# A graph attention layer and a mixture of experts on one core: another order of one step's work in the attention stage

## The chip, the cores and the metric

The kernel runs as one program on one core of a Trainium2 chip. The core has TensorE (PE: matmuls, with a separate path for loading weights, PEld), VectorE (DVE), ScalarE (ACT), GpSimd (POOL) and SyncE (SP, which here issues all the DMAs). Each engine works through its own queue in the order in which it was written, and semaphores tie the queues together. The metric is the device time of one execution in microseconds.

## The reference, cut to what matters

The input is 128 graphs of 128 nodes with 256 features each, and a weighted adjacency matrix for each graph. All is float32.

```
x = x + gnn(layernorm(x), adj, W, a)
x = x + ffn(layernorm(x), ...)

gnn: Wh = h @ W;  s1 = Wh @ a1;  s2 = Wh @ a2
     e = leaky_relu(s1[i] + s2[j], 0.2) + log(adj + 1e-6)
     h' = softmax(e) @ Wh

ffn: w = softmax(mean over graphs(h) @ Wr + br)          # 8 experts
     for each expert: relu(bn(h @ W1 + b1)), relu(bn(. @ W2 + b2)), . @ Wo + bo
     y = sum of the experts' results, weighted by w
```

## The kernel before, in words

The program has two stages. The first, the attention stage, goes through 32 groups of four graphs and leaves x + h' of each group in a buffer in device memory. The second goes through the same groups as tiles of 512 rows and computes the eight experts. The change touches the first stage alone.

In the attention stage each engine runs the function `step(g, layer)` for g from -1 to 33 in a software pipeline. In step g the engines work on several groups: `nxt` is group g+1, g itself, `a` is group g-1, `b` is g-2, `t` is g-3 and `h` is g-4. The journey of one group is this:

- `nxt`: TensorE transposes its rows (L774, into `ps_th`), ScalarE copies them (`xnT`, L530). VectorE takes the mean and variance of each row (`stats_1`, L559, aggregated at L573), and GpSimd makes the reciprocal deviation (L399, L403).
- g: TensorE projects (`project`, L726, into `ps_wide`), ScalarE copies with the deviation as scale (`wh`, L512). TensorE spreads the score of each node over the partitions (L765, into `ps_s`), ScalarE adds the other score (`s_sb`, L520).
- `a`: VectorE makes the leaky ReLU (`l_sb`, L617) and the negated row maximum (L627), ScalarE the exponential (`e_sb`, L504), VectorE the product with the adjacency matrix (`p_sb`, L661) and its row sums (L674).
- `b`: TensorE transposes p_sb (L737, into `ps_pT`), ScalarE copies it (`pT`, L497), TensorE multiplies it with wh (the attention product, L755, into `ps_th`), and VectorE divides by the row sums and adds the rows of x (`x1`, L647). It then takes the statistics of the new rows (L567).
- `t` and `h`: the statistics are aggregated (L578), GpSimd makes the deviation (L433, L436), and the normalised rows are summed over the groups in `acc`, which is `resb`: two of the four graphs on VectorE (`add_part`, L604), two on GpSimd (`x1s_high` L442, and the addition L446).

The rows of x, transposed, and the attention product use the same PSUM tensor (`ps_th`), and the two copies of wh alternate between groups, so that the copy of wh of group g overwrites the wh that the attention product of group g-2 reads.

The order of the work is written out by hand in `step` of each engine. Three ranges of steps differ in what they do on the side. Steps -1 to 5 and 30 to 33 are unrolled and do nothing else. Steps 6 to 21 (`layer == 1`, a loop of pairs) prepare the first weights of one expert in each pair: in the even step SyncE loads W1 into `w_stage` and GpSimd makes four sums of blocks of it (L455 to L462); in the odd step ScalarE copies them to a rounded form (`wq_hi`, L541) and GpSimd takes the rest (`wq_lo`, L467). Steps 22 to 29 (`layer == 2`) prepare the second weights, one expert in each step: SyncE loads W2 (L366) into one half of `w_stage`, ScalarE copies it (`w_hi`, L545), GpSimd takes the rest (`w_lo`, L472).

SyncE issues in step g: the rows of x of group g+2 (L326, which wait for the transposes and the row statistics of group g), the store of group g-3 (L347), the rows of x of group g-1 once more, for the sum (L352), the adjacency matrices of group g (L355), and the weights if there are any.

Of the kernel before, what the change touches and what calls it, by code (L numbers as in the profile page):

```python
# [24 lines left out]
P = 128  # L25
# [13 lines left out]
def adj_ffn(nc, x, adj, gnn_w, gnn_a, wr, br, w1, b1, g1, be1, m1, v1, w2, b2, g2, be2, m2, v2, wo, bo, out):  # L39
# [17 lines left out]
    with ExitStack() as ctx:  # L57
# [127 lines left out]
        with ExitStack() as sa:  # L185
# [296 lines left out]
            def _(act):  # L482
# [8 lines left out]
                def step(g, layer):  # L491
                    p = g[1]
                    b = ago(g, 2)
                    if exists(b):
                        act.wait_ge(pT_ready, num(b) + 1)
                        wait(act, h_ready, num(b))
                        nc.scalar.activation(pT[:, :, :], ps_pT[:, :, :], ACT.Copy).then_inc(pT_copied, 1)  # L497
                    a = ago(g, 1)
                    if exists(a):
                        act.wait_ge(neg_m_done, num(a) + 1)  # L500
                        wait(act, p_done, num(a))

                        for b4 in range(GB):
                            last = nc.scalar.activation(e_sb[:, b4, :], l_sb[:, b4, :], ACT.Exp,  # L504
                                                        bias=neg_m[:, b4:b4 + 1])
                        last.then_inc(e_done, 1)
                    if exists(g):
                        act.wait_ge(wh_ready, num(g) + 1)
                        act.wait_ge(rstd1_done, num(g) + 1)
                        wait(act, h_ready, num(g) - 1)  # L510
                        for b4 in range(GB):
                            last = nc.scalar.activation(wh[p][:, b4, :], ps_wide[:, b4, 0:D + 2], ACT.Copy,  # L512
                                                        scale=rstd1[p][:, b4:b4 + 1])
                        last.then_inc(wh_copied, 1)
                    nxt = ago(g, -1)
                    if exists(g):
                        act.wait_ge(s2b_ready, num(g) + 1)
                        wait(act, l_done, num(g))
                        for b4 in range(GB):
                            last = nc.scalar.activation(s_sb[:, b4, :], ps_s[:, b4, :], ACT.Identity,  # L520
                                                        bias=wh[p][:, b4, D:D + 1])
                        last.then_inc(s_done, 1)
                    if is_step(g, BN_STEP - 1):
                        act.wait_ge(bn_T, 1)
                        nc.scalar.activation(bn_in[:, :, :, :].rearrange("p l i k -> p (l i) k"), ps_bn,
                                             ACT.Copy).then_inc(bn_copied, 1)
                    if exists(nxt):
                        act.wait_ge(xnT_ready, num(nxt) + 1)
                        wait(act, wh_ready, num(nxt))
                        nc.scalar.activation(xnT[:, :, :], ps_xT, ACT.Copy).then_inc(xnT_copied, 1)  # L530
                    t = ago(g, 3)
                    if exists(t) and not is_step(t, G - 1):
                        act.wait_ge(stats2_done, num(t) + 1)
                        nc.scalar.activation(mean_all[:, num(t), :], mv2[t[1]][:, :, 0],
                                             ACT.Copy).then_inc(mean2_done, 1)
                    if is_step(g, G):
                        tile_copy(act, 0, ps_x0)
# [4 lines left out]
                    if layer == 2:  # L542
# [3 lines left out]
                                             w_half[p], ACT.Copy).then_inc(w_hi_done, 1)  # L546

# [5 lines left out]
            def _(dve):  # L553
# [31 lines left out]
                def step(g, layer):  # L585
# [23 lines left out]

                    if exists(b):  # L610
                        dve.wait_ge(rowsum_done, num(b) + 1)
# [12 lines left out]
                    add_part(0)  # L624
# [4 lines left out]
                    add_part(1)  # L629
# [23 lines left out]
                    if exists(nxt):  # L653
                        wait(dve, rstd1_done, num(nxt) - 1)
                        stats_1(nxt, 0)
                        stats_1(nxt, 1)
# [7 lines left out]
                    if exists(nxt):  # L664
                        stats_1(nxt, 2)
                        stats_1(nxt, 3)
# [32 lines left out]
            def _(pe):  # L699
# [30 lines left out]
                def step(g, layer):  # L730
                    b = ago(g, 2)
                    nxt = ago(g, -1)
                    if exists(b):
                        pe.wait_ge(p_done, num(b) + 1)
                        wait(pe, pT_copied, num(b))
                        for b4 in range(GB):
                            last = nc.tensor.transpose(ps_pT[:, b4, :], p_sb[:, b4, :], ident[:, :])  # L737
                        last.then_inc(pT_ready, 1)
                    if is_step(g, G):
                        pe.wait_ge(wh_copied, G)  # L740
                        tile_transpose(pe, 0, ps_x0)
                    if is_step(g, 0):
                        pe.wait_ge(va_copied, 1)
                    if exists(g):
                        pe.wait_ge(xnT_copied, num(g) + 1)
                        wait(pe, wh_copied, num(g))
                        project(g, range(GB)).then_inc(wh_ready, 1)
# [530 lines left out]
```

## Time and profile before

| what | value |
|---|---|
| median of three runs | 2516.02 us (2515.35 to 2516.1) |
| the profiled execution's own time | 2515.62 us |
| its span | 2513.8 us |
| PE busy | 2397.0 us (95%) |
| DVE busy | 1729.6 us (69%) |
| ACT busy | 1596.0 us (63%) |
| POOL busy | 453.7 us (18%) |
| attention stage | from the start to about 370 us |

The busy times are sums over the whole span, of which the attention stage is about a seventh, so they say little about it; its own steps have to be read from the timeline. In the rows of the timeline a line gives the start, the duration, the engine, the line of the kernel, the instruction, what it writes and reads, and how many instructions in succession were merged into the row. A bracket at the end gives the time that the engine sat idle before the row, and what ended it. A row of windows gives the stretch, its length, the busy time and instructions of PE, PEld, DVE, ACT and POOL, and then TensorE's granted clock, the DMA engines' busy share and GB/s.

### The profile page before, as it was taken

What the parts mean: (1) busy time and instruction counts of PE and PEld (TensorE: products, weight loads), DVE (VectorE), ACT (ScalarE), POOL (GpSimd) and SP (SyncE); (2) the same over time, 40 slices, a digit from 0 to 9 for tenths busy, and PEclk for the clock granted to TensorE, in tenths of its full rate; (3) what the DMA queues carried; (4) which work ended last, traced back from release to release, by engine and by line L of the source; (5) the groups of instructions that cost most, each with busy time, mean ns of one, the idle gap of its engine ahead of it and who ended that gap; (6) DMA issues with size and microseconds to landing.
All of it is one profiled execution on the core that took longest, in us unless ns stands there. A gap on an engine that the chain in (4) does not pass through costs nothing.

```text
span 2513.8 us, 45142 instructions
## 1 busy us (share of the span) xinstructions
PE 2397.0 (95%) x16308; PEld 2209.6 (88%) x16308; DVE 1729.6 (69%) x2445; ACT 1596.0 (63%) x2465; POOL 453.7 (18%) x423
## 2 busy tenths in 40 slices
PE   6777769999999999999999999999999999999999
PEld 5666648999999999999999999999999999999998
DVE  4888875666666666666666666666666666666665
ACT  3555545666666666666666666666666666666665
POOL 3566642111101110111111111111111001101110
PEclk9999988999999999999999999999999999999999
DMA  4555641000000000000000000000000000000000
GB/s 136 192 187 187 199 133 43 26 26 25 25 25 25 23 19 23 18 18 25 25 25 25 25 25 25 25 25 25 25 25 25 25 25 25 17 25 17 17 18 26
DMA packets 91179, 116.16 MB, mean 46 GB/s; under 512 B 4701, under 2 KB 78857, under 8 KB 91145
## 3 DMA queue, kind: packets, MB, share of 16 engines
q1 hardware_dynamic: 91144, 115.73, 14.0%
q8 instruction: 19, 0.31, 0.1%
q14 instruction: 16, 0.12, 0.0%
HBM read 82.16 MB, written 33.55 MB: 46 GB/s over the span
## 4 chain that ended last, share of the span: by engine, by line
PE 84%; DVE 1%; ACT 0%; issue 0%; ACTq 0%
PE ps_y L1178 29%; PE ps_wide L171 29%; PE ps_wide L1160 26%; PE ps_t L132 1%; DVE h_lo L1065 0%; DVE h L1072 0%; PE ps_y L1226 0%; DVE z L1058 0%; ACT v L972 0%; DVE h_lo L1080 0%; ACT h_hi L986 0%; ACT h_hi L967 0%; ACT w_bc L1014 0%; ACT h L980 0%; DVE z L1048 0%
## 5 line engine op out<-in xcount | busy, mean ns | idle before, releaser
L972 ACT ACTIVATE v<-ps_wide,bn_cols 128x256 f32<-128x256 f32 x768 | 434.6, 566 | 399.1 <-PE ps_wide L1160 272.1
L980 ACT ACTIVATE h<-ps_wide,bn_cols 128x512 f32<-128x512 f32 x512 | 399.3, 780 | 328.4 <-PE ps_wide L171 328.4
L1178 PE MATMUL ps_y<-wo_lo,h_hi 128*128 128x256 f32 x2048 | 578.8, 283 | 0.0
L1178 PE MATMUL ps_y<-wo_hi,h_hi 128*128 128x256 f32 x2048 | 577.1, 282 | 1.6 <-DVE h_lo L1080 1.6
L1178 PE MATMUL ps_y<-wo_hi,h_lo 128*128 128x256 f32 x2048 | 578.3, 282 | 0.0
L1160 PE MATMUL ps_wide<-xq_hi,wq_hi 128*128 128x256 f32 x1792 | 505.9, 282 | 11.9 <-PEq L185 8.4
L1160 PE MATMUL ps_wide<-xq_lo,wq_hi 128*128 128x256 f32 x1792 | 509.5, 284 | 0.0
L1160 PE MATMUL ps_wide<-xq_hi,wq_lo 128*128 128x256 f32 x1792 | 506.8, 283 | 0.0
L1080 DVE TENSOR_TENSOR h_lo<-h,h_hi 128x1024 fp32r<-128x1024 f32 x256 | 318.1, 1243 | 241.6 <-ACT h_hi L986 241.6
L1058 DVE SCALAR_TENSOR_TENSOR z<-ps_wide,bn_cols,v 128x512 f32<-128x512 f32 x256 | 192.0, 750 | 319.3 <-PE ps_wide L1160 319.3
L171 PE MATMUL ps_wide<-h_hi,w_hi 128*128 128x512 f32 x1024 | 404.8, 395 | 2.1 <-DVE h_lo L1065 2.1
L171 PE MATMUL ps_wide<-h_lo,w_hi 128*128 128x512 f32 x1024 | 405.9, 396 | 0.0
L171 PE MATMUL ps_wide<-h_hi,w_lo 128*128 128x512 f32 x1024 | 405.9, 396 | 0.0
L1065 DVE SCALAR_TENSOR_TENSOR h_lo<-z,h_hi 128x1024 fp32r<-128x1024 f32 x256 | 316.3, 1235 | 117.9 <-ACT h_hi L967 117.9
L1178 PEld LDWEIGHTS ps_y<-wo_hi,h_hi 128*128 128x128 f32 x2048 | 386.5, 189 | 1.9 <-DVE h_lo L1080 1.8
L1178 PEld LDWEIGHTS ps_y<-wo_hi,h_lo 128*128 128x128 f32 x2048 | 387.4, 189 | 0.0
L1178 PEld LDWEIGHTS ps_y<-wo_lo,h_hi 128*128 128x128 f32 x2048 | 386.4, 189 | 0.1
L950 POOL TENSOR_TENSOR resb<-resb,bias_out 128x1024 f32<-128x1024 f32 x32 | 85.6, 2674 | 1535.2 <-DMA resb<-x_scratch 1535.2
L1160 PEld LDWEIGHTS ps_wide<-xq_hi,wq_hi 128*128 128x128 f32 x1792 | 340.9, 190 | 24.6 <-issue 9.4
L1160 PEld LDWEIGHTS ps_wide<-xq_hi,wq_lo 128*128 128x128 f32 x1792 | 338.2, 189 | 10.0
L1160 PEld LDWEIGHTS ps_wide<-xq_lo,wq_hi 128*128 128x128 f32 x1792 | 339.8, 190 | 0.0
L1072 DVE TENSOR_TENSOR h<-h,w_bc 128x1024 f32<-128x1024 f32 x256 | 313.1, 1223 | 7.5 <-ACT w_bc L1014 4.7
(131 smaller groups left out, 3059.4 us busy)
## 6 DMA issues: line engine op xcount, KB each, us to landing
x_sb<-in_x SPq DMA_DIRECT2D x32, 512.0 KB, 3.9
res<-in_x SPq DMA_DIRECT2D x32, 512.0 KB, 5.8
x1t<-x_scratch SPq DMA_DIRECT2D x32, 512.0 KB, 3.3
resb<-x_scratch SPq DMA_DIRECT2D x32, 512.0 KB, 3.3
out<-resb SPq DMA_DIRECT2D x32, 512.0 KB, 3.0
adj_sb<-in_adj SPq DMA_DIRECT2D x32, 256.0 KB, 6.0
x_scratch<-h SPq DMA_DIRECT2D x16, 512.0 KB, 4.7
x_scratch<-w_bc SPq DMA_DIRECT2D x16, 512.0 KB, 4.5
```

What stands on the lines that cost most here:

```text
L132: last = nc.tensor.transpose(ps_x[:, c, b4 * N:(b4 + 1) * N], x1t[:, b4, c * P:(c + 1) * P], ident[:, :])
L171: mm = nc.tensor.matmul(acc_ps, w[:, i, c, cols], s[:, c, :], start=start and n == 0, stop=stop and n == len(terms) - 1)
L950: nc.gpsimd.tensor_tensor(resb[:, :, :], resb[:, :, :], bias_out[:, None, :].to_broadcast([P, GB, D]), ALU.add).then_inc(resb_done, 1)
L972: nc.scalar.activation(v[:, slot, :], ps_l1[:, 0, 0:H], ACT.Identity, bias=bn_cols[:, 1, cols], scale=bn_cols[:, 0, cols]).then_inc(done, 1)
L980: nc.scalar.activation(h2[:, m, :], ps_l2[:, m, :], ACT.Relu, bias=bn_cols[:, 3, cols], scale=bn_cols[:, 2, cols]).then_inc(r2_done, 1)
L1058: nc.vector.scalar_tensor_tensor(out=z[:, 0, :], in0=ps_l1[:, 1, :], scalar=bn_cols[:, 0, C * e:C * e + 1], in1=v[:, 0:2, :].rearrange("p ...
L1065: nc.vector.scalar_tensor_tensor(out=h1_lo[:, :, :], in0=z[:, :, :], scalar=0.0, in1=h1_hi[:, :, :].bitcast(F32), op0=ALU.max, op1=ALU.sub ...
L1072: nc.vector.tensor_tensor(h2w[:, :, :].rearrange("p c (b n) -> p (c b) n", n=N), h2[:, :, :].rearrange("p c (b n) -> p (c b) n", n=N), w_b ...
L1080: nc.vector.tensor_tensor(h2_lo[p][:, :, :], h2w[:, :, :], h2_hi[p][:, :, :].bitcast(F32), ALU.subtract).then_inc(lo2_done, 1)
L1160: mm = nc.tensor.matmul(out_ps, w[:, e, q, :], x[:, q, :], start=start and n == 0, stop=stop and n == len(terms) - 1, skip_group_check=True)
L1178: mm = nc.tensor.matmul(ps_y[:, b4, :], h[:, c, cols], w[:, e, c, :], start=(e == 0 and k == 0 and b4 % per_bank == 0), stop=(e == E - 1 a ...
```

## The change

In the attention stage the queues of TensorE, ScalarE and VectorE get another order in `step`. No instruction is added or taken away, and the other queues stay as they are.

- TensorE had: transposes of p_sb (of group g-2), projection, attention product, spread scores, transposes of the next rows. It now has: attention product (g-2), projection (g), transposes of the next rows (g+1), spread scores (g), and last the transposes of p_sb, now of group g-1.
- ScalarE had: pT (g-2), exp (g-1), wh (g), s (g), xnT (g+1), the means, weights. It now has: s (now of group g-1), the weights, exp (g-1), the means, wh (g), xnT (g+1), and last pT (now of group g-1).
- VectorE has both additions to `acc` at the head of the step, ahead of the leaky ReLU, and all four row statistics of the next group behind p_sb.

```
# TensorE, step
-                    if exists(b):
-                        pe.wait_ge(p_done, num(b) + 1)
-                        wait(pe, pT_copied, num(b))
-                        ... transposes of p_sb into ps_pT ...
                     if exists(b):
                         pe.wait_ge(pT_copied, num(b) + 1)
-                        pe.wait_ge(wh_copied, num(b) + 1)
                         wait(pe, x1_done, num(b))
                         ... attention product ...
+                    if exists(g):
+                        ... project(g) ...
+                    if exists(nxt):
+                        pe.wait_ge(x_loaded[nxt[1]], 16 * (nxt[0] + 1))
+                        for c in range(C):
+                            wait(pe, (x1_low_done, x1_done)[c], num(b) + 1)
+                            ... transposes of the next rows ...
                     if exists(g):
                         ... spread scores ...
-                    if exists(nxt):
-                        ... transposes of the next rows ...
+                    if exists(a):
+                        pe.wait_ge(p_done, num(a) + 1)
+                        wait(pe, pT_copied, num(a))
+                        ... transposes of p_sb into ps_pT ...
# ScalarE, step
-                    if exists(b):
-                        ... pT ...
                     a = ago(g, 1)
+                    if exists(a):
+                        act.wait_ge(s2b_ready, num(a) + 1)
+                        wait(act, l_done, num(a))
+                        ... s_sb, with wh of a ...
+                    if layer == 1 and p == 1:
+                        ... wq_hi, behind wq_sum ...
+                    if layer == 2:
+                        act.wait_ge(w2_loaded[p], 16 * (g[0] - K1 + 1))
+                        ... w_hi ...
                     if exists(a):
                         ... e_sb ...
+                    ... mean_all ...
                     if exists(g):
                         ... wh ...
-                    if exists(g):
-                        ... s_sb, with wh of g ...
                     if exists(nxt):
                         ... xnT ...
-                    ... mean_all, wq_hi, w_hi ...
+                    if exists(a):
+                        act.wait_ge(pT_ready, num(a) + 1)
+                        wait(act, h_ready, num(a))
+                        ... pT ...
# VectorE, step
+                    add_part(0)
+                    add_part(1)
                     ... l_sb, rinv, aggregate_2 ...
-                    add_part(0)
                     ... neg_m ...
-                    add_part(1)
                     ... x1 ...
-                    stats_1(nxt, 0), stats_1(nxt, 1)
                     ... p_sb ...
-                    stats_1(nxt, 2), stats_1(nxt, 3)
+                    stats_1(nxt, 0) to stats_1(nxt, 3)
                     ... stats_2, rowsum, aggregate_1 ...
```

## Rows read from the trace of the kernel before

**Rows 1.** Timeline of VectorE: p_sb in steps 1, 6, 29 and 32.
```profile
29.17 0.69 DVE L661 SCALAR_TENSOR_TENSOR p_sb<-adj_sb,e_sb 128x512 f32<-128x512 f32 x1 [0.69 <-ACT e_sb L504]
...
85.50 0.67 DVE L661 SCALAR_TENSOR_TENSOR p_sb<-adj_sb,e_sb 128x512 f32<-128x512 f32 x1
...
326.69 0.68 DVE L661 SCALAR_TENSOR_TENSOR p_sb<-adj_sb,e_sb 128x512 f32<-128x512 f32 x1
...
354.66 1.47 DVE L661 SCALAR_TENSOR_TENSOR p_sb<-adj_sb,e_sb 128x512 f32<-128x512 f32 x1
```
**Rows 2.** Timeline of TensorE, steps 16 and 17.
```profile
190.39 1.16 PE L765 MATMUL ps_s<-ident,wh 128*128 128x128 f32 x8 [1.67 <-ACT wh L512]
...
191.38 1.04 PE L774 MATMUL ps_th<-ident,x_sb 128*128 128x128 f32 x8
...
192.25 0.60 PE L737 MATMUL ps_pT<-ident,p_sb 128*128 128x128 f32 x4
...
193.69 3.76 PE L726 MATMUL ps_wide<-gw,xnT 128*128 128x258 f32 x16 [0.84 <-ACT xnT L530]
...
197.29 1.89 PE L755 MATMUL ps_th<-wh,pT 128*128 128x256 f32 x8
```
**Rows 3.** Timeline of ScalarE in the same stretch.
```profile
191.58 1.15 ACT L520 ACTIVATE s_sb<-ps_s,wh 128x128 f32<-128x128 f32 x4 [1.25 <-PE ps_s L765]
...
193.60 0.62 ACT L497 ACTIVATE pT<-ps_pT 128x512 f32<-128x512 f32 x1
...
196.12 1.28 ACT L504 ACTIVATE e_sb<-l_sb,neg_m 128x128 f32<-128x128 f32 x4 [1.89 <-DVE neg_m L627]
...
199.30 1.58 ACT L512 ACTIVATE wh<-ps_wide,rstd 128x258 f32<-128x258 f32 x4 [1.91 <-PE ps_th L755]
```
**Rows 4.** Timeline of VectorE from p_sb of step 16 to that of step 17.
```profile
190.48 0.67 DVE L661 SCALAR_TENSOR_TENSOR p_sb<-adj_sb,e_sb 128x512 f32<-128x512 f32 x1
...
194.07 0.69 DVE L617 SCALAR_TENSOR_TENSOR l_sb<-s_sb 128x512 f32<-128x512 f32 x1
...
195.03 0.45 DVE L604 SCALAR_TENSOR_TENSOR resb<-w_bc,rstd_all,resb 128x256 f32<-128x256 f32 x1
...
196.00 0.61 DVE L604 SCALAR_TENSOR_TENSOR resb<-w_bc,rstd_all,resb 128x256 f32<-128x256 f32 x1
...
198.45 1.66 DVE L647 SCALAR_TENSOR_TENSOR w_bc<-ps_th,rinv,res 128x256 f32<-128x256 f32 x4 [1.84 <-PE ps_th L755]
...
200.69 0.72 DVE L661 SCALAR_TENSOR_TENSOR p_sb<-adj_sb,e_sb 128x512 f32<-128x512 f32 x1
```
**Rows 5.** Timeline of GpSimd, and one addition of VectorE, in steps 16 to 18.
```profile
194.45 0.63 POOL L455 TENSOR_TENSOR w_stage<-w_stage 128x128 f32<-128x128 f32 x1
...
196.41 0.52 POOL L462 TENSOR_TENSOR w_stage<-w_stage 128x128 f32<-128x128 f32 x1
...
198.47 1.04 POOL L442 TENSOR_TENSOR x1s_high<-h,rstd_all 128x512 f32<-128x512 f32 x1 [0.18 <-POOL rstd_all L436]
...
205.31 2.08 POOL L467 TENSOR_TENSOR wq_lo<-w_stage,wq_hi 128x896 f32 x1 [0.59 <-ACT wq_hi L541]
...
205.39 2.29 DVE L604 SCALAR_TENSOR_TENSOR resb<-h,rstd_all,resb 128x256 f32<-128x256 f32 x1
```
**Rows 6.** SyncE's first and last issue in step 25, w_stage's landings, w_hi.
```profile
276.60 0.37 SPq L326 DMA_DIRECT2D x_sb<-in_x  x1
...
279.84 0.42 SPq L366 DMA_DIRECT2D w_stage<-in_L_ffn_W  x1
...
DMA to landing us min/median/max: 3.7/5.3/5.8
...
288.14 0.65 ACT L545 ACTIVATE w_hi<-w_stage 128x512 f32 x1
```
**Rows 7.** TensorE's transposes of p_sb in step 33, and that stretch by windows.
```profile
356.19 1.11 PE L737 MATMUL ps_pT<-ident,p_sb 128*128 128x128 f32 x4 [3.21 <-DVE p_sb L661]
...
356.00:362.00 6.00, 4.89 (x12) 3.24 (x12) 4.32 (x16) 0.80 (x2) 3.10 (x5) 0.50 0.16 65
```

More of the change, by code:

```diff
@@ L507, in step @@
-                    if exists(g):
[L508 to L514, printed above, removed]
@@ L531, in step @@
[L531 to L537, printed above, removed]
                     if layer == 1 and p == 1:
@@ L664, in step @@
                     if exists(nxt):
-                        stats_1(nxt, 2)
-                        stats_1(nxt, 3)
+                        wait(dve, rstd1_done, num(nxt) - 1)
+                        for b4 in range(GB):
+                            stats_1(nxt, b4)
                     if with_stats:
@@ L759, in step @@
                         last.then_inc(h_ready, 1)
+                    if is_step(g, 0):
+                        pe.wait_ge(va_copied, 1)
+                    if exists(g):
+                        pe.wait_ge(xnT_copied, num(g) + 1)
+                        wait(pe, wh_copied, num(g))
+                        project(g, range(GB)).then_inc(wh_ready, 1)
+                    if is_step(g, G):
+                        pe.wait_ge(wh_copied, G)
+                        tile_transpose(pe, 0, ps_x0)
+                    if exists(nxt):
+                        pe.wait_ge(x_loaded[nxt[1]], 16 * (nxt[0] + 1))
+                        for c in range(C):
+                            wait(pe, (x1_low_done, x1_done)[c], num(b) + 1)
+                            for b4 in range(GB):
+                                last = nc.tensor.transpose(ps_xT[:, c, b4 * N:(b4 + 1) * N],
+                                                           x_sb[nxt[1]][:, b4, c * P:(c + 1) * P], ident[:, :])
+                        last.then_inc(xnT_ready, 1)
                     if exists(g):
@@ L767, in step @@
                         last.then_inc(s2b_ready, 1)
-                    if exists(nxt):
-                        pe.wait_ge(x_loaded[nxt[1]], 16 * (nxt[0] + 1))
-                        wait(pe, xnT_copied, num(nxt))
-                        for c in range(C):
-                            wait(pe, (x1_low_done, x1_done)[c], num(b) + 1)
-                            for b4 in range(GB):
-                                last = nc.tensor.transpose(ps_xT[:, c, b4 * N:(b4 + 1) * N],
-                                                           x_sb[nxt[1]][:, b4, c * P:(c + 1) * P], ident[:, :])
-                        last.then_inc(xnT_ready, 1)
+                    if exists(a):
+                        pe.wait_ge(p_done, num(a) + 1)
+                        wait(pe, pT_copied, num(a))
+                        for b4 in range(GB):
+                            last = nc.tensor.transpose(ps_pT[:, b4, :], p_sb[:, b4, :], ident[:, :])
+                        last.then_inc(pT_ready, 1)
                     if is_step(g, BN_STEP - 1):
```

69 lines of the change are left out of this document (31 added, 38 removed).

## The prediction

> **What bounds the kernel now.** I read the page first: the slices show the attention stage in the first seventh of the span (the change touches nothing else), and the chain of waits lies almost wholly in the stage behind it, so it doesn't price this change. I then read the timeline of two neighbouring steps in the middle of the stage, engine by engine, and last what the DMA queue and GpSimd do in the steps that also load weights. I mark a step by the start of its product p_sb (L661): 85.50 us in step 6, 326.69 in step 29, so 23 steps took 241.2 us, 10.49 each [rows 1].
>
> One step closes a loop through TensorE and ScalarE [rows 2, 3]: projection to the start of the attention product 3.60 us (193.69 to 197.29), product 1.89, then the copies of wh 1.58, which wait for that product (its wait is printed on the row), the broadcast 1.16, and the copies of s and xnT 2.11 (191.58 to 193.69, where the projection starts, its wait for xnT printed on the row); with 0.2 of hand-overs 10.54. VectorE is a near second: from p_sb at 190.48 to the next at 200.69 it waited only 1.84, for the product [rows 4]. So 8.2 us of its own work stand in a lap (3.59 to l_sb, then 6.62 less 1.84 and less 0.16 that one addition lost).
>
> **The change, part by part.** Times below are counted from T, the start of a step's attention product.
>
> TensorE's order. Nothing is added. The product goes first and its pT was copied in the step before, so wh no longer waits for a product behind the projection. Lap: product 1.73 of its 1.89 (the next instruction starts before the last one ends, as the 0.99 from 190.39 to 191.38 of 1.16 show), projection 3.76, wh copies 1.58 (the transposes of the next rows, 0.87, lie beside them), broadcast 0.99 to the first transpose of the product, transposes 0.60, copy of pT 0.62 [rows 2, 3], four hand-overs 0.18: 9.46. The copies of s now run at the head of the next step beside the product, xnT's copy beside the broadcast, and neither is waited for. That is 1.08 less than 10.54. What is late next is VectorE: its transposes need p_sb at T+8.15.
>
> VectorE's order. The two additions (0.45 each, 0.4 apart) now stand ahead of l_sb, the four row statistics behind p_sb. The moves cost no instruction. l_sb starts at T+1.1 (s ready), the maximum and x1 follow (1.93 to the second addition, less the first, 0.4; then 1.6), so p_sb is reached 3.1 after l_sb, T+4.2; exp, 1.28 after the maximum, is hidden by x1 [rows 3, 4]. x1 is done at T+4.2, before the row transposes want it (T+5.3). The reserve toward T+8.15 is 3 us, and toward the wh copies behind exp on ScalarE 1.3.
>
> The port that VectorE and GpSimd share. An addition of 0.45 took 2.29 beside GpSimd's wq_lo (2.08), and ended 0.29 after it [rows 4, 5]: of two instructions one waits for the other's end. In the new order p_sb meets GpSimd's x1s_high (1.04), which starts 1.5 after GpSimd turns to the aggregated variance (196.93 to 198.47), l_sb+2.6 to +3.65. So p_sb loses between 0 and 1.04; I take 0.35, nearest to these starts. VectorE's lap is then 8.55, below 9.46: plain steps run at 9.46. From p(0) at 29.2 (unchanged, [rows 1]): wh 1.6, broadcast 1.0, transposes 0.6, copy 0.7, so T of step 2 is 33.15; four laps of 9.46 later step 6 has T 71.0 and p_sb at 75.4, 10.1 earlier than now.
>
> Steps 6 to 21 (one W1 expert per pair). GpSimd reaches its weight work 3.97 after p_sb (190.48 to 194.45); with two statistics (0.65, 2.24 less x1's 1.6) now behind p_sb, 4.62 [rows 4, 5]. VectorE's second addition starts at p_sb+4.65 and l_sb wants to at 5.05. In the odd step that weight work is wq_lo, 2.08: the addition or l_sb waits it out, so l_sb starts at p_sb+6.85. In the even step it is the first of four sums, about 0.3: l_sb at p_sb+5.25. Their end, 2.1 after l_sb's start (196.93 less 194.07 is 2.9 today, with both additions between), releases wq_hi (0.97, estimated from w_hi's 0.65 for 512 columns against 896), which now stands ahead of exp: exp ends 4.4 after l_sb and p_sb starts at 4.5. GpSimd, freed by the same sum, is then just ending x1s_high. A pair is odd 4.5+6.85, even 3.45+5.25, together 20.05 against 20.97 now; VectorE is the bound, TensorE's 18.92 is hidden. Both ends: 18.92 (all hidden) and 22.4 (GpSimd's addition behind x1s_high, 1.2 by an estimate from the 1.04 of that one, also goes ahead of p_sb, once in each step). 15 steps at 10.0: p_sb of step 21 at 225.4 against 242.8.
>
> Steps 22 to 29 (one W2 expert each): here the change loses. ScalarE's w_hi stood at the end of its step (288.14), on weights whose load was issued at 279.84; its median landing is 5.3, so it had 3.0 of cover [rows 6]. It now stands behind s, at T+1.1, ahead of exp, wh, xnT and pT. SyncE issues that load last of five in its step, 3.24 behind the load of x_sb (276.60), and x_sb's load waits for the row statistics, now behind p_sb. So a loop closes: p_sb 0.67, four statistics 1.35, hand-over to SyncE 0.2 (an estimate), four issues 3.24, landing 5.3, w_hi 0.65, exp 1.28, hand-overs 0.14: 12.8 us, against 10.49. That the engines idle in it changes nothing. Its ends: landing 3.7 (the one issued apart from the others) gives 11.2, landing 5.8 gives 13.3. I take 5.3, since the four transfers ahead on the same queue are unchanged. The first of the eight is issued behind wq_lo instead (p_sb+7.3) and lands in 3.7: 13.0 with w_hi and exp. p_sb of step 29: 225.4+13.0+7*12.8=328.0 against 326.7.
>
> TensorE's clock in these steps. Now its longest wait in a step is 1.67 [rows 2]. In the new loop the row transposes end at T+6.3 and the broadcast starts after exp and wh, T+10.5: 4.2 us idle in 12.8. After 3.21 us of idleness four transposes took 1.11 instead of 0.60 and the granted clock was 0.50, the 1.2 GHz level [rows 7]. One step at that level costs the others nothing, since p_sb hangs on the load with 4 us in reserve; only the broadcast and transposes of step 29 (1.6 at full clock, 0.85 of that more) would pass on: 0 to 1.4, and I take 1.4. The Trainium skill (TensorE: Matmul & The Clock Gate, section "Why this matters for your kernels") says that idle gaps between bursts of matmuls bring back the half clock, which speaks against this change: by it the drop is certain, and the steps behind would start slow too (about what the second rival gives). The trace agrees in kind [rows 7].
>
> The end. Behind step 29: 3.9 to T of step 30, two laps of 9.46, and 4.4 to p_sb of step 32: 27.2, against 28.8 now (354.66 plus 0.80 by which its 1.47 exceed 0.67, less 326.69). Two additions (0.8) come ahead of the aggregation from which the stage's end hangs. So 328.0+27.2+0.8-355.5=0.5, and the clock's 1.4: +1.9 us.
>
> The profiled execution took 2515.62 (span 2513.8), 0.4 below the median 2516.02. 2515.6+1.9+0.4=2518.
>
> **The rivals.**
> 1. The W2 load is less in the way: the loop of steps 22 to 29 takes 11.2 with the 3.7 landing. For it: the queue has longer pauses between bursts. Against: the burst in front of the load is the same four transfers. 8*1.6=12.8 less: 2505, faster.
> 2. TensorE falls to the half clock in steps 22 to 29 and stays there for several. For it: 4.2 us of idleness against the 3.21 of [rows 7]. Against: at half clock TensorE would be busy nearly throughout, which should bring the clock back. Its lap would be (1.73+3.76+0.99+0.60)*1.85+2.4=15.5, 2.7 over the loop; in five of eight steps 13: 2531, slower. It decides from the point where the late TensorE exceeds p_sb's reserve, after two such steps.
> 3. GpSimd wins the port in each step, its addition as well as x1s_high running ahead of p_sb: VectorE's lap is 9.75 in plain steps (1 in all), and 1.2 more in each of 15: 2537, slower. Against it: at wq_lo's end (207.39) the waiting VectorE instruction went ahead and ended at 207.68 [rows 5].
> 4. The change doesn't shorten the plain laps (s at the head of ScalarE's step runs into something unseen): 10 lost, 2528. Little speaks for it.
>
> **How the numbers follow.** Forecast 0.52, own range 2511 to 2525; rivals 0.24, 0.15, 0.06, 0.03. Two gains of about 10 and 7 us are set against a loss of 19, so the sign is open; 0.2% (5 us) is about what this kernel's measurement tells from no change. The forecast gives 0.08 faster, 0.28 same, 0.16 slower; rival 1 gives 0.22 faster and 0.02 same, the others slower but 0.01. So faster 0.30, same 0.31, slower 0.39. The range is 2503 to 2534: below by rival 1 with a little more from the port, above by rival 2.
>
> **What would show it.** p_sb 9.4 to 9.5 apart in steps 3 to 6; about 20 us per pair in steps 6 to 21, with l_sb (or an addition) of 2 us and more beside wq_lo; 12.8 apart in steps 22 to 29, with w_hi and exp waiting for the DMA of w_stage; x_sb's issues right behind the statistics. Wrong if w_hi doesn't wait, if TensorE's clock is 0.50 through those steps, or if p_sb takes over 1.5 us in most steps.

## The result, and the profile after

The kernel after took 2512.56 us (median of 20 runs, 2510.76 to 2516.51), the kernel before beside it 2516.59 (20 runs, 2515.29 to 2518.15): ratio 0.9985 with a 95% interval of 0.9979 to 0.9992. It is faster by 4 us, where 1.9 slower was forecast. The profiled execution of after took 2514.45 (span 2512.7), 1.2 less than that of before. The rest of the 4 us is scatter of single executions, which is wider than before (5.8 us from lowest to highest, against 2.9): the profiled execution of after lies 1.9 above its median, that of before 1.0 below. The profiled executions of stats_ahead, stats_ahead_warm and adds_back, further down, lie 4.4 below, 4.8 above and 2.5 above their medians, so a difference of a few us between two rows of the table can be scatter.

The small sum hides two large terms. I take them from the starts of p_sb (now L656), which is the mark the prediction uses. In the timeline of VectorE, steps 21, 22, 29 and 30 of after (start us, duration, engine, line, operation, and in brackets the idle time before it and what ended it):

```profile
219.01 0.83 DVE L656 SCALAR_TENSOR_TENSOR p_sb<-adj_sb,e_sb 128x512 f32<-128x512 f32 x1 [1.19 <-ACT e_sb L515]
...
231.54 0.69 DVE L656 SCALAR_TENSOR_TENSOR p_sb<-adj_sb,e_sb 128x512 f32<-128x512 f32 x1 [4.35 <-ACT e_sb L515]
...
325.17 0.69 DVE L656 SCALAR_TENSOR_TENSOR p_sb<-adj_sb,e_sb 128x512 f32<-128x512 f32 x1 [3.92 <-ACT e_sb L515]
...
334.56 0.98 DVE L656 SCALAR_TENSOR_TENSOR p_sb<-adj_sb,e_sb 128x512 f32<-128x512 f32 x1
```

With the same marks of every kernel run for this study (us of its profiled execution, all starts of p_sb, read from timelines; step 29 and 32 of before are [rows 1]):

```
                  step 21    21 to 29 (a lap)   29 to 32   step 32
before             242.69     84.00 (10.50)      27.97     354.66
forecast           225.4     102.6  (12.8)       27.2+1.4  356.6
after              219.01    106.16 (13.27)      28.25     353.42
w_hi_last          219.25     75.73  (9.47)      27.60     322.58
stats_ahead        221.70     89.65 (11.21)      29.07     340.42
load_first         219.48     82.03 (10.25)      28.24     329.75
adds_back          236.68    102.50 (12.81)      32.93     372.11
warm               218.81    104.16 (13.02)      28.17     351.14
stats_ahead_warm   221.96    100.05 (12.51)      27.00     349.01
dve_only           242.79     83.99 (10.50)      28.45     355.23
wq_early           217.85     76.88  (9.61)      27.61     322.34
pe_act_only        226.50     97.13 (12.14)      31.70     355.33
adds_back_wq       221.88    102.82 (12.85)      31.71     356.41
load_fourth        219.78     99.09 (12.39)      29.94     348.81
```

After has gained 23.7 us by step 21, and has lost 22.2 of it again by step 29.

**Plain steps.** TensorE and the two copies that end its waits, step 3 to 4 of after:

```profile
41.76 1.99 PE L736 MATMUL ps_th<-wh,pT 128*128 128x256 f32 x8 [0.69 <-ACT pT L543]
...
43.60 3.65 PE L722 MATMUL ps_wide<-gw,xnT 128*128 128x258 f32 x16
...
47.29 1.58 ACT L528 ACTIVATE wh<-ps_wide,rstd 128x258 f32<-128x258 f32 x4 [0.90 <-PE ps_wide L722]
...
48.91 1.16 PE L763 MATMUL ps_s<-ident,wh 128*128 128x128 f32 x8 [0.79 <-ACT wh L528]
...
49.91 0.60 PE L770 MATMUL ps_pT<-ident,p_sb 128*128 128x128 f32 x4
...
50.55 0.60 ACT L543 ACTIVATE pT<-ps_pT 128x512 f32<-128x512 f32 x1 [0.77 <-PE ps_pT L770]
...
51.20 0.48 PE L736 MATMUL ps_th<-wh,pT 128*128 128x256 f32 x1 [0.69 <-ACT pT L543]
```

Each row starts within 0.2 us of where the one above ends, product to product 9.44 (51.20 less 41.76). This is the lap that the prediction added up from the rows of before. The starts of p_sb are 9.0 to 9.4 apart in laps 4 to 6, since VectorE has reserve and its own mark moves inside TensorE's lap.

**Steps 6 to 21.** From step 9 on the starts of p_sb repeat every four laps (8.11, 9.69, 10.35, 10.07, in all 38.22, 9.56 each); over all fifteen laps they are 9.66 apart, while TensorE's products are 9.55 apart (70.14 in step 6, 213.38 in step 21), so that p_sb slides 1.6 us back inside TensorE's lap. Two neighbouring odd steps differ. GpSimd, VectorE and TensorE, steps 14 to 16:

```profile
165.51 2.26 POOL L467 TENSOR_TENSOR wq_lo<-w_stage,wq_hi 128x896 f32 x1
...
165.59 1.99 PE L736 MATMUL ps_th<-wh,pT 128*128 128x256 f32 x8 [0.76 <-ACT pT L543]
166.52 1.79 DVE L618 SCALAR_TENSOR_TENSOR l_sb<-s_sb 128x512 f32<-128x512 f32 x1 [0.70 <-ACT s_sb L498]
...
175.17 1.99 PE L736 MATMUL ps_th<-wh,pT 128*128 128x256 f32 x8 [0.76 <-ACT pT L543]
...
184.72 1.99 PE L736 MATMUL ps_th<-wh,pT 128*128 128x256 f32 x8 [0.77 <-ACT pT L543]
185.03 0.86 DVE L603 SCALAR_TENSOR_TENSOR resb<-h,rstd_all,resb 128x256 f32<-128x256 f32 x2
185.58 2.86 POOL L467 TENSOR_TENSOR wq_lo<-w_stage,wq_hi 128x896 f32 x1
185.81 0.68 DVE L618 SCALAR_TENSOR_TENSOR l_sb<-s_sb 128x512 f32<-128x512 f32 x1
```

In one, l_sb stands beside wq_lo and takes 1.79 instead of 0.68. In the other l_sb takes 0.68 and it is wq_lo that takes longer, 2.86. TensorE's products are 9.58 and 9.55 apart in spite of both, each waiting only for pT: VectorE's delays don't reach them. The 0.1 over the plain lap lies in the hand-overs (0.76 before the product instead of 0.69).

**Steps 22 to 29.** What was waited for on each engine, 220 to 330 us (us in total, times, longest):

```profile
ACT w_hi L508 <- DMA w_stage<-in_L_ffn_W: 48.1, 8, 7.1
...
DVE p_sb L656 <- ACT e_sb L515: 32.0, 8, 4.7
PEld ps_s L763 <- ACT wh L528: 26.1, 9, 5.3
```

The chain from one p_sb to the next, timeline of step 22 to 23 (SPq are SyncE's issues):

```profile
232.15 1.40 DVE L558 BATCH_NORM_STATS2 st<-x_sb 128x6 f32<-128x256 f32 x4
...
233.78 0.37 SPq L326 DMA_DIRECT2D x_sb<-in_x  x1
...
237.00 0.47 SPq L366 DMA_DIRECT2D w_stage<-in_L_ffn_W  x1
...
243.49 0.63 ACT L508 ACTIVATE w_hi<-w_stage 128x512 f32 x1 [7.11 <-DMA w_stage<-in_L_ffn_W]
244.02 1.26 ACT L515 ACTIVATE e_sb<-l_sb,neg_m 128x128 f32<-128x128 f32 x4
245.31 0.69 DVE L656 SCALAR_TENSOR_TENSOR p_sb<-adj_sb,e_sb 128x512 f32<-128x512 f32 x1 [4.66 <-ACT e_sb L515]
246.88 2.08 PE L763 MATMUL ps_s<-ident,wh 128*128 128x128 f32 x8 [5.07 <-ACT wh L528]
```

That is the loop of the prediction, here 13.77 long: the row statistics release x_sb's load, SyncE issues the W2 load 3.2 later, and this landed 6.4 after its issue, not 5.3. In the seven full laps (22 to 29) every other part is fixed within 0.4 us: 2.2 from p_sb to x_sb's issue, 3.2 to 3.6 to the W2 load's issue, 1.83 from w_hi to the next p_sb. Only the time from that issue to w_hi moves, 5.3 to 7.0, 6.0 on average. The last row also shows TensorE at its lower level of 1.2 GHz, 2.08 for what takes 1.16, behind 5.07 of idleness. By windows (start:end, length, busy time of TensorE, its weight loads, VectorE, ScalarE and GpSimd, granted clock, DMA share, GB/s):

```profile
80.00:225.00 145.00, 121.00 (x670) 102.93 (x670) 131.46 (x412) 89.66 (x236) 110.09 (x130) 1.00 0.64 205
238.00:330.00 92.00, 67.74 (x298) 56.34 (x296) 58.33 (x189) 40.13 (x108) 41.82 (x49) 0.80 0.51 164
```

No engine is near full in the second window, and neither are the DMA engines over a whole lap (0.51): a chain of waits sets the time there. One link of it, the landing, is the length of a burst, in which the DMA engines are busy (last section).

### The profile page after: what moved, and what is told of

Its sections match the earlier page's. It is cut to its first block, busy times and chain, and to the rows that moved or that the text cites. A ratio compares the mean times of both kernels' runs of the same rounds, so it can differ in the third digit from the quotient of the medians.

```text
span 2512.7 us, 45085 instructions
## 1 busy us (share of the span) xinstructions
PE 2410.9 (96%) x16308; PEld 2222.2 (88%) x16308; DVE 1717.6 (68%) x2445; ACT 1594.9 (63%) x2465; POOL 459.1 (18%) x423
## 4 chain that ended last, share of the span: by engine, by line
PE 84%; DVE 1%; ACT 0%; issue 0%; ACTq 0%
PE ps_y L1173 29%; PE ps_wide L171 29%; PE ps_wide L1155 26%; PE ps_t L132 1%; DVE h_lo L1060 0%; DVE h L1067 0%; PE ps_y L1221 0%; DVE z L1053 0%; ACT v L967 0%; DVE h_lo L1075 0%; ACT h_hi L981 0%; ACT h_hi L962 0%; ACT w_bc L1009 0%; ACT h L975 0%; DVE z L1043 0%
```

## Experiments

I had two questions. Is the loss in steps 22 to 29 the place of w_hi, or TensorE's clock? And what sets the laps up to step 21: VectorE with the port (my theory), or TensorE's loop? Ratios are to the kernel before on the same chip, with 95% intervals. All kernels compute the whole reference.

**w_hi_last**: after, with w_hi back at the end of ScalarE's step.

```
# ScalarE, step
-   ... w_hi, behind s_sb ...
    ... e_sb, mean_all, wh, xnT, pT ...
+   ... w_hi ...
```

> The changed kernel with the copy w_hi (W2 steps, 22 to 29) back at the end of ScalarE's step; all else as changed. Theory (load loop: the load of w_stage, w_hi, exp, p_sb, row statistics, the issue of x_sb's load, three more issues, the load): the wait of w_hi for the DMA goes from 48 us in eight steps to about 0, the p_sb of steps 22 to 29 come 9.4 to 9.7 apart instead of 13.3, TensorE's granted clock is 1.00 there, and the kernel takes 8*3.7=29 us less than the changed one: about 2484. Rival (the loss in these steps comes from VectorE and GpSimd meeting at the port, w_lo beside l_sb): w_lo is still there, laps stay above 12, about 2510.

Measured: 2485.10 (2483.32 to 2486.34, 4 runs), ratio 0.9877 [0.986, 0.9893]. Laps of 9.47 in steps 22 to 29, a granted clock of 1.00 (228 to 304 us), and no wait for the DMA of w_stage is left. The timeline of step 25 to 26:

```profile
262.78 0.47 SPq L366 DMA_DIRECT2D w_stage<-in_L_ffn_W  x1
...
270.69 0.62 ACT L542 ACTIVATE w_hi<-w_stage 128x512 f32 x1
```

The load has 7.9 us before it is wanted, more than the 5.4 median (6.0 at most) that it takes. So the place of this one copy costs 27 us of the change, and everything else in it is a gain of 31. This is the fastest order found, with wq_early within the scatter of it.

**stats_ahead**: after, with the four row statistics ahead of p_sb, so that x_sb's load is released earlier.

```
# VectorE, step
    ... x1 ...
+   stats_1(nxt, 0) to stats_1(nxt, 3)
    ... p_sb ...
-   stats_1(nxt, 0) to stats_1(nxt, 3)
```

> The changed kernel with the four row statistics ahead of p_sb; w_hi stays ahead of exp. Load-loop theory: the issue of x_sb's load no longer hangs on p_sb but on TensorE's row transposes, so the loop runs over two steps: exp's end to the next T 3.9, to the transposes' end 6.3, issue 0.2, three more issues 3.24, landing 5.5, w_hi 0.65, exp 1.28: 21.1 in two steps, 10.5 per lap in steps 22 to 29 instead of 13.3; w_hi still waits for the DMA. 22 us less than the changed kernel, about 2491. Rival (the half clock of TensorE makes these laps long): the clock would have to stay low, laps 12 and more, above 2505.

Measured: 2505.71 (2501.33 to 2506.85, 5 runs), 0.9957 [0.9943, 0.9971]. The sign was right and the size wrong: laps from 9.86 to 13.26, mean 11.21. Two of the eight were long (13.16 and 13.26), and in the lap ahead of each TensorE's product took 3.78 instead of 1.99 (236.21 and 260.24). Row transposes and x_sb's issue came late behind it, 2.6 and 3.1 after p_sb, where in the other full laps the issue lay between 1.1 ahead of p_sb and 0.6 behind it. The second of the two, by the timeline of step 24 to 25:

```profile
256.21 0.69 DVE L660 SCALAR_TENSOR_TENSOR p_sb<-adj_sb,e_sb 128x512 f32<-128x512 f32 x1 [2.16 <-ACT e_sb L515]
258.43 0.46 SPq L366 DMA_DIRECT2D w_stage<-in_L_ffn_W  x1
260.24 3.78 PE L736 MATMUL ps_th<-wh,pT 128*128 128x256 f32 x8 [0.76 <-ACT pT L543]
...
264.66 0.63 ACT L508 ACTIVATE w_hi<-w_stage 128x512 f32 x1 [3.51 <-DMA w_stage<-in_L_ffn_W]
```

The half clock is thus a second suspect for the long laps; warm and stats_ahead_warm take that up.

**load_first**: after, with SyncE issuing the W2 load first in its step, not last.

```
# SyncE, step
+   ... W2 load into w_half[p], with its two waits ...
    ... x_sb, x_scratch, res, adj_sb ...
-   ... W2 load ...
```

> The changed kernel, but SyncE issues the load of W2 first in its step instead of last; w_hi stays ahead of exp. Load-loop theory: the load no longer waits for the row statistics nor stands behind four other transfers, so it has landed before w_hi wants it: laps of 9.4 to 9.7 in steps 22 to 29, about 2484, as with w_hi at the end. Rival (w_hi's place on ScalarE ahead of exp is what costs, load or no load): laps stay above 12, about 2510.

Measured: 2490.79 (2489.27 to 2492.11, 4 runs), 0.9898 [0.9882, 0.9915]. Behind the first three laps (12.65, 9.87, 11.51) the laps are 9.5 to 9.7, and w_hi waited once, 6.0 us, where it waited 8 times for 48.1. With the load early, w_hi may stay where the change put it. The 7 us over my 2484 are those first laps. The first load can only be issued once wq_lo has freed w_stage (227.40), so w_hi waited 6.0 for it. TensorE, idle for 3.94 meanwhile, then ran at its lower level (the broadcast 2.08 at 233.69, the projection 4.46 at 240.96, granted clock 0.76 and 0.81 in 226 to 238 and 238 to 250 us), and the copy of wh waited 3.93 for that projection: here slow matmuls do stand in the way, for some 1.6 us (laps 9.87 and 11.51 against 10.22 and 9.52 in w_hi_last).

**adds_back**: after, with the two additions in their old places, behind aggregate_2 and behind neg_m.

```
# VectorE, step
-   add_part(0)
-   add_part(1)
    ... l_sb, rinv, aggregate_2 ...
+   add_part(0)
    ... neg_m ...
+   add_part(1)
    ... x1 ...
```

> The changed kernel with the two additions to acc in their old places, behind the aggregation and behind the maximum. Theory (in steps 3 to 21 TensorE's own loop of 9.44 us sets the lap and VectorE has about 1 us of reserve in each): the additions now stand between l_sb and p_sb, p_sb moves 0.8 later in its step and still comes before its transposes; laps in steps 6 to 21 stay within 9.5 to 9.7, steps 22 to 29 stay at 13.3; within 3 us of the changed kernel, 2510 to 2516. Rival (VectorE and the port set the lap in steps 6 to 21): wq_lo then meets two additions ahead of the maximum instead of one instruction, laps grow by 0.4 or more on average, 2519 and more.

Measured: 2531.12 (2528.44 to 2533.66, 4 runs), 1.0055 [1.0039, 1.0072], slower than both kernels and outside what my theory gave; the rival that priced the additions' place higher held. The laps of steps 6 to 21 are 10.68 long. Timeline of adds_back:

```profile
177.30 2.08 POOL L467 TENSOR_TENSOR wq_lo<-w_stage,wq_hi 128x896 f32 x1
177.38 2.54 DVE L616 SCALAR_TENSOR_TENSOR l_sb<-s_sb 128x512 f32<-128x512 f32 x1 [0.54 <-ACT s_sb L498]
...
182.77 1.35 PE L755 MATMUL ps_th<-ident,x_sb 128*128 128x128 f32 x8 [0.85 <-DVE h L646]
```

In every pair wq_lo starts ahead of l_sb, which loses 0.8 to 1.9 (here 1.85). With an addition on each side of neg_m, x1 then comes so late that TensorE's row transposes wait for it: here VectorE does set TensorE's pace. At the head of the step the additions run while VectorE would wait for s, and l_sb comes off wq_lo in every second pair.

**dve_only**: before, with VectorE's new queue alone.

```
# VectorE, step: additions to the head, all four statistics behind p_sb, as in after
# TensorE and ScalarE: as in before
```

> The kernel before, with only VectorE's new order (both additions at the head of the step, the four row statistics behind p_sb); TensorE and ScalarE as before. Theory (before, TensorE and ScalarE's loop of 10.54 sets the lap and VectorE waits in it for the product): laps stay 10.4 to 10.6, w_hi doesn't wait for the load; 2514 to 2519. Rival (the gain in steps 6 to 21 comes from VectorE's order by itself): laps of 10.1 or less there, 2510 or less.

Measured: 2515.83 (10 runs), 0.9997 [0.9987, 1.0006], laps of 10.49 and 10.50. Alone it does nothing, since the old loop through TensorE and ScalarE (10.54 by [rows 2, 3]) stays.

**pe_act_only**: the counterpart, TensorE's and ScalarE's new orders with VectorE's old queue.

```
# VectorE, step: additions at their old places, two statistics ahead of p_sb, two behind, as in before
# TensorE and ScalarE: as in after
```

> The new order on TensorE and ScalarE alone; VectorE's queue as in the kernel before (additions behind the aggregation and behind the maximum, two of the row statistics ahead of p_sb). Theory (the shorter loop of TensorE pays in steps 6 to 21 only with the additions at the head of VectorE's step, as the kernel with the additions back showed): laps there 10.4 to 10.8, in steps 22 to 29 11.5 to 13 with w_hi waiting for the load; 2520 to 2532, slower than before. Rival (the additions' place matters only together with the statistics behind p_sb): laps of 9.8 or less in steps 6 to 21, 2512 or less.

Measured: 2516.25 (10 runs), 1.0000 [0.999, 1.0009]. Of my numbers only the laps of steps 22 to 29 (12.14) held: 2520 to 2532 was too slow, and so were laps of 10.4 to 10.8, where 9.95 were measured. The rival's 9.8 and 2512 were not reached either. By the marks it gained 16.2 by step 21 (laps of 9.10 and 10.80), lost 13.1 in steps 22 to 29 and 3.7 behind them, +0.7 in all. Its loss in the load loop is smaller than that of after (97.13 against 106.16), as two statistics ahead of p_sb release x_sb's load earlier. Timeline:

```profile
170.91 2.08 POOL L467 TENSOR_TENSOR wq_lo<-w_stage,wq_hi 128x896 f32 x1
171.65 1.89 DVE L616 SCALAR_TENSOR_TENSOR l_sb<-s_sb 128x512 f32<-128x512 f32 x1 [1.20 <-ACT s_sb L498]
```

Behind step 29 a term shows that the prediction doesn't have. With the additions on both sides of neg_m the four normalisations of x1t (L124), which follow in step 31, take 3.1 us (before, pe_act_only, adds_back and adds_back_wq), with the additions at the head 1.4 (after). Why isn't shown.

pe_act_only and adds_back differ only in two row statistics, ahead of p_sb or behind it, and are 15 us apart (2516.25 and 2531.12); l_sb loses 1.2 beside wq_lo in the one and 1.9 in the other, but I didn't follow the rest.

So the whole change's 4 us are not the sum of its parts (0 and 0): VectorE's new queue is worth 0 on the old loop and 4 on the new one (7.5 by step 21).

**adds_back_wq**: adds_back, with wq_lo moved on GpSimd from behind the four sums to ahead of rstd_1, where VectorE has no l_sb.

```
# GpSimd, step (beside the edit of adds_back)
    ... x1s_high, addition ...
+   ... wq_lo ...
    ... rstd_1, transform of the weights ...
-   ... wq_lo ...
```

> The kernel with the additions back (2531.1, laps of 10.68 in steps 6 to 21, l_sb 2.5 us beside wq_lo in every pair), with GpSimd's wq_lo ahead of the deviation of the next rows, where VectorE runs the row statistics. Theory (the port makes the difference: additions between l_sb and x1 leave l_sb to meet wq_lo): no l_sb over 1 us, laps of 9.9 or less in steps 6 to 21, 2519 or less. Rival (x1 comes 0.8 later because of the additions themselves, and the row transposes and wh wait for it): laps stay at 10.3 or more, 2525 or more.

Measured: 2517.88 (10 runs), 1.0006 [0.9997, 1.0016], laps of 9.77 in steps 6 to 21, step 21 at 221.88 instead of adds_back's 236.68. Of these 14.8 us 1.3 were there at step 6, ahead of any wq_lo, so taking the meeting of l_sb and wq_lo away is worth 13.5 us in fifteen laps. l_sb took 1.00 at most, and theory and number held: where VectorE is late, the meeting counts.

**wq_early**: w_hi_last, with the same move of wq_lo.

```
# GpSimd, step (beside the edit of w_hi_last): wq_lo ahead of rstd_1
```

> The kernel with w_hi at the end of ScalarE's step (2485.1), and with GpSimd's wq_lo ahead of the deviation of the next rows instead of behind it, so that it runs beside the row statistics and not beside l_sb. Theory (in steps 6 to 21 TensorE's loop of 9.44 is the bound, and the port costs 0.2 per lap through l_sb's 1.8 us in every fourth step): no l_sb of over 1 us, laps 9.44 to 9.5 on average, 3 us less: 2482. Rival (VectorE's own work, not the port, holds the laps at 9.66): laps unchanged, 2485.

Measured: three runs of 2483.6 to 2488.1 (a fourth took 4776 and isn't counted), 0.9885 [0.9865, 0.9904], no better than w_hi_last. l_sb never took over 0.70:

```profile
165.71 1.99 PE L736 MATMUL ps_th<-wh,pT 128*128 128x256 f32 x8 [0.77 <-ACT pT L538]
166.64 0.69 DVE L618 SCALAR_TENSOR_TENSOR l_sb<-s_sb 128x512 f32<-128x512 f32 x1 [0.78 <-ACT s_sb L498]
...
175.29 1.99 PE L736 MATMUL ps_th<-wh,pT 128*128 128x256 f32 x8 [0.76 <-ACT pT L538]
176.40 0.69 DVE L618 SCALAR_TENSOR_TENSOR l_sb<-s_sb 128x512 f32<-128x512 f32 x1 [1.13 <-ACT s_sb L498]
...
184.79 1.99 PE L736 MATMUL ps_th<-wh,pT 128*128 128x256 f32 x8 [0.76 <-ACT pT L538]
```

Its laps are 9.95 and 9.13, 9.54 each, against 9.56 with the meetings; the products stand 9.58 and 9.50 apart. Taking the suspected bound away moved the settled lap by 0.02 us, and TensorE's products by 0.01 (9.54 apart from step 6 to 21, against 9.55 in after and w_hi_last). p_sb of step 21 does come 1.4 us earlier than in w_hi_last, as it no longer slides back inside TensorE's lap, but that is reserve and not time. My 2482 and the rival's 2485 are too close for three runs to tell apart. This is the run that fells "VectorE is the bound": TensorE's loop is.

**warm**: after, with TensorE repeating the transposes of the next rows four times in steps 22 to 29. The repeats write the same values to the same place, so what changes is its idle time.

```
-    for b4 in range(GB):
+    for b4 in [q for _ in range(4 if layer == 2 else 1) for q in range(GB)]:
```

> The changed kernel; in steps 22 to 29 TensorE does the transposes of the next rows four times over (the same values, some 2.6 us more work per step), so that it doesn't sit idle behind them. It tells what the half clock costs there. Theory (the load loop sets these laps and holds no TensorE instruction): granted clock 1.00 in these steps instead of 0.80, laps still 12.6 to 14, the kernel within 3 us of the changed one, 2510 to 2515. Rival (the half clock lengthens the laps): they fall to 12 or less, 2503 or less.

Measured: 2512.87 (10 runs), 0.9989 [0.9979, 0.9998], the time of after. Windows and timeline of warm:

```profile
238.00:330.00 92.00, 79.14 (x477) 69.51 (x476) 62.20 (x193) 41.44 (x112) 43.09 (x50) 0.93 0.52 166
```

```profile
241.20 3.65 PE L755 MATMUL ps_th<-ident,x_sb 128*128 128x128 f32 x32
243.37 0.63 ACT L508 ACTIVATE w_hi<-w_stage 128x512 f32 x1 [6.58 <-DMA w_stage<-in_L_ffn_W]
...
246.77 1.16 PE L763 MATMUL ps_s<-ident,wh 128*128 128x128 f32 x8 [1.91 <-ACT wh L528]
```

The granted clock is 0.93 instead of 0.80 and the broadcast is back at 1.16, yet w_hi waits as long and the laps are 13.02. The laps are 0.25 shorter than after's, but that isn't the clock: from w_hi to p_sb it takes 1.83 in both kernels, and from p_sb to x_sb's issue 2.2 but for one lap. What is shorter is the time from the W2 load's issue to w_hi, 5.5 on average instead of 6.0. Inside this loop the half clock costs nothing that can be seen.

**stats_ahead_warm**: both edits, to see whether the long laps of stats_ahead were the clock's.

> The kernel with the row statistics ahead of p_sb (laps of 10.3 and 13.3 in turn where 10.5 was expected, with slow matmuls in the long ones), with the same repeated transposes in steps 22 to 29. In it the loop of the load runs through TensorE. Theory (the half clock is what made every second lap long): the clock stays at 1.00, all laps 10.6 to 12 (the repeated transposes stand in the loop only where the row transposes do, up to 2.6 per two steps), no lap of 13; the kernel takes 2500 to 2505, not more than stats_ahead's 2505.7. Rival (the long laps come from the landing of the load): they stay at 13 and the kernel takes 2508 or more.

Measured: 2508.95 (6 runs), 0.9978 [0.9963, 0.9993], laps from 10.64 to 15.54 with a granted clock of 0.96. By the time the rival held (2508 or more). The run doesn't settle the question, though: it didn't keep the clock up where that matters (a product of 3.77 at 252.16, ahead of the lap of 15.54), landings reached 7.1 us, and the row transposes, 3.65 instead of 1.04, stand ahead of x_sb's issue in each lap. In both kernels the long laps are those in which this issue comes more than 2 us behind p_sb; how much of that is the clock's stays open.

**load_fourth**: after, with the W2 load issued ahead of adj_sb's, fourth instead of last. It asks whether a load lands a fixed time after its issue, or when the bytes ahead of it are through.

```
# SyncE, step
    ... x_sb, x_scratch, res ...
+   ... W2 load ...
    ... adj_sb ...
-   ... W2 load ...
```

> The changed kernel with the load of W2 issued fourth in SyncE's step, ahead of adj_sb (0.25 MB, whose issue takes 1.3 us) instead of behind it. The load loop predicts shorter laps in steps 22 to 29, and by how much tells what the load waits for. If it lands a fixed 5.5 us behind its issue: laps 13.0-1.55=11.5, 12 us less, 2501. If it lands when the bytes in front of it are through (0.25 of 2 MB fewer in a burst at about 370 GB/s): laps 13.0-0.7=12.3, 6 us less, 2507. Rival (the load is not in the loop): no change, 2512.

Measured: 2507.67 (2505.1 to 2511.69, 5 runs), 0.9968 [0.9954, 0.9982], laps of 12.39. The load's issue starts 1.5 us earlier behind x_sb's (1.84 against 3.31) and has 256 KB less ahead of it, and the lap is 0.9 shorter by the profiled executions and 0.6 by the medians (4.9 us in eight laps), nearer to the 0.7 of the bytes ahead than to the 1.55 of a fixed time. The row of w_stage's landings says the same: median 6.2 here against 5.5 in after, an issue nearer to the head of the burst and a longer way from it. One rival this run doesn't exclude: the fourth issue takes 1.1 us in either order, so the load's issue ends only 0.8 earlier, and a fixed time behind that end would give much the same lap. Against it speak the landings in the last section.

```profile
DMA to landing us min/median/max: 2.8/6.2/7.3
```

## Why the prediction was wrong

The time, 2512.56, lies in the range; the sign of the forecast was wrong. To the first product of the next stage (370.19 in before, 368.80 in after) the forecast was +1.9, so 372.1, and 3.3 of error remain:

- **Plain laps of 9.46**: right, 9.44, row by row. With the first steps, step 6 stood at 74.17 instead of 75.4, 1.2 too late in the forecast (0.2 of it a slip of mine: T 71.0 and 4.2 more are 75.2).
- **"VectorE is the bound, TensorE's 18.92 is hidden"**: this step failed. A pair was to take 20.05 and took 19.11 (twice 9.56), worth 5.2 over 15 steps, 6.4 together with the 1.2. (p_sb's fifteen laps took 144.8 instead of 150.0, TensorE's products 143.2.) Three rows show why VectorE's sum came out too long. Only every second l_sb of an odd step meets wq_lo ahead of it, and it loses 1.1, not 1.8 (1.79 at 166.52). In the other, l_sb goes ahead of a wq_lo that was already issued (185.58 and 185.81). And exp waited for wq_hi only in every second odd step (1.19 at 219.01). The delays that are left stand beside TensorE's loop; wq_early shows it: with them gone TensorE's products are 0.01 us a lap closer. I had both ends (18.92 and 22.4 for a pair) and took the middle: but a delay in one lap of an engine with reserve (3 us by my own sum) is absorbed, and only the mean over the pattern had to stay under TensorE's. My own mean for VectorE was too high because I charged each odd step with the full meeting.
- **The load loop of 12.8**: right in mechanism, sized too low. Measured 13.27 a lap, 106.16 instead of 102.6, +3.6 (the first lap took 12.53, forecast 13.0). The term that was off is the landing: 5.3, the median of before [rows 6], where the load of the first full lap of after took 6.4 and the longest 6.8 (median 5.5). w_hi_last shows that this wait, with what follows from it, is the whole loss. Most of the 3.6 may belong to this one execution: its second, third and fourth load took 6.4 to 6.8, and from the issue to w_hi it took 6.0 us on average, where the four other kernels with the same order of issues and the same place of w_hi (warm, adds_back, adds_back_wq, pe_act_only) took 5.5 each. With 5.5 the loop would be 12.9, by estimate, close to the forecast; that the median execution gained 4.0 where the profiled one gained 1.2 fits this. The term that then carries the sign is the one above.
- **Rival 1 (a loop of 11.2)**: no. It asked for a landing of 3.7 behind four transfers. Only the first load, issued 3.6 us behind the transfer before it, landed that early (2.6); the seven others took 5.2 or more.
- **Rival 2 (half clock for several steps)**: the clock did fall, to 0.80 over these steps, but w_hi's wait covers it, as warm shows, and no lap came near 15.5. What I priced at 1.4 on leaving the loop is there: the broadcast and the transposes of step 29 took 2.00 and 1.06 instead of 1.16 and 0.60, 1.3 more.

```profile
326.74 2.00 PE L763 MATMUL ps_s<-ident,wh 128*128 128x128 f32 x8 [3.78 <-ACT wh L528]
328.52 1.06 PE L770 MATMUL ps_pT<-ident,p_sb 128*128 128x128 f32 x4
```

  The Trainium skill (TensorE: Matmul & The Clock Gate, section "Why this matters for your kernels") has gaps bring back the half clock; the trace agrees, with 2.08 instead of 1.16 at 246.88.
- **Rivals 3 and 4**: neither. p_sb took 0.98 in plain steps (0.3 lost at the port, 0.35 forecast), and the plain laps did shorten.
- **The end, 0.8 for the two additions**: in part. The aggregation (L577) starts 2.70 behind the end of the last p_sb instead of 2.11, and from that end to the next stage's first product it takes 14.39 instead of 14.06, 0.3 more. From p_sb of step 29 to the next stage's first product 43.63, forecast 44.1, before 43.50.

So -6.4, +3.6 and -0.5 make the -3.3. The sign hung on the first two, each larger than the forecast's 1.9. The prediction called the sign open and gave the faster side 0.30; that the time falls in its range comes of the load loop, which it had right, and of the width of the range.

## What to carry to other kernels

A reordered queue is worth the mean of its slowest loop, not the sum of each engine's delays: add up each engine's lap over a whole repeat of the pattern, and count a delay only where it exceeds the reserve before the next hand-over. Before a copy that waits for a transfer is moved forward in its queue, compare the cover between issue and use with the landing in its burst: with landings of 5.2 to 6.8 us, one place in a queue turned a gain of 31 us into one of 4. Try the parts of an order apart and together, since here they were worth 0 each and 4 together, with one misplaced copy hiding the rest.

## What the runs showed of the hardware

- **Who gets the port.** A wq_lo issued at 185.58, 0.23 ahead of l_sb, took 2.86 instead of 2.08, as if it waited for l_sb to end (l_sb took its usual 0.68), though in other steps l_sb waited for wq_lo. What differs in the rows: at 185.58 two additions of VectorE (185.03 to 185.89) were running, and l_sb followed them at once; at 165.51 VectorE then waited 0.70 for s_sb. It looks as if VectorE kept the port from one instruction to the next behind it. That is an inference from these rows; no run isolates it. The Trainium skill (SBUF — State Buffer, section "Who interferes with whom") has a VectorE instruction with two SBUF inputs, as these are, contend with a GpSimd instruction that reads SBUF, and lets the order of issue decide who blocks. The rows at 165.51 agree; those at 185.58 agree only if the port counts as held by the additions and is then passed on within VectorE's queue.
- **A load lands with its burst.** Of the eight W2 loads of after, 256 KB each, the first, issued 3.6 us behind the last of the other four transfers of its step, took 2.6 us; the seven issued right behind them took 5.2 to 6.8. The whole burst, in the DMA view of after from 231 to 246 us (packets and bytes of the window, then each issue with its time to landing):

```profile
DMA packets 2002, 2.11 MB, mean 141 GB/s; under 512 B 80, under 2 KB 1872, under 8 KB 2000
...
x_sb<-in_x SPq DMA_DIRECT2D x1, 512.0 KB, 4.1
x_scratch<-h SPq DMA_DIRECT2D x1, 512.0 KB, 5.1
res<-in_x SPq DMA_DIRECT2D x1, 512.0 KB, 6.1
adj_sb<-in_adj SPq DMA_DIRECT2D x1, 256.0 KB, 7.3
w_stage<-in_L_ffn_W SPq DMA_DIRECT2D x1, 256.0 KB, 6.4
```

  The issues of the first four are 0.6 us apart (233.78 to 235.46), but they land 1.5 to 1.8 apart (237.9, 239.4, 241.0, 242.8), in the order of issue, and the load last of all. From x_sb's issue (233.78) to the last landing (243.4) 2.1 MB took 9.6 us, and this, not any one transfer's own time, is the length that the loop contains.
